# Four attention layers on one core: layer 1's neighbour rows fetched by an indirect DMA instead of one-hot products

## The reference, cut to what matters

```python
q = split(rmsnorm(x_tokens, gamma_q) @ Wq.T)              # 16 heads of 16
kn = rmsnorm(ctx, gamma_kv)
k, v = split(kn @ Wk.T), split(kn @ Wv.T)
mask = abs(ctx_pos - ctx_index_per_token) <= 1            # three rows per token
w = square(relu(q . k / 4)), zero outside the mask
out = (w / max(sum(w), 1e-6)) @ v
return x_tokens + out @ Wo.T
```

## Time and profile before

| | |
|---|---|
| median of three runs | 1463.18 us |
| the profiled execution | 1463.84 us |
| its span in the trace | 1462.0 us |
| TensorE busy | 1306.4 us, 89% |
| VectorE busy | 958.3 us, 66% |
| ScalarE busy | 779.8 us, 53% |
| GpSimd busy | 356.7 us, 24% |
| chain that ended last | TensorE 72%, VectorE 19%, ScalarE 4% |
| memory traffic | mean 20 GB/s over the span |

### The profile page before, as it was taken

How to read it: one execution, slowest core, us unless ns; L and a number is a source line. 1 busy time by engine, 2 the same in 40 slices (tenths; PEclk the granted TensorE clock), 3 DMA queues, 4 the chain that set the end, 5 groups by cost and what they waited for, 6 DMA issues and landing times.

```text
span 1462.0 us, 26277 instructions
## 1 busy us (share of the span) xinstructions
PE 1306.4 (89%) x9618; PEld 1027.6 (70%) x9618; DVE 958.3 (66%) x1908; ACT 779.8 (53%) x2690; POOL 356.7 (24%) x782
## 2 busy tenths in 40 slices
PE   3667889999999999999999999999999999888755
PEld 2345667877777787778777777877787777776533
DVE  2446567768686867777686768677776868573522
ACT  1133556657565646566575656464665656464411
POOL 1112303232322213132323232131323232302020
PEclk9779999999999999999999999999999999999855
DMA  6700000000000000000000000000000000000000
GB/s 205 282 1 13 3 12 2 17 4 16 4 16 4 9 11 0 20 0 16 4 16 4 16 4 9 11 0 20 0 16 4 16 4 4 4 5 5 4 4 4
DMA packets 23967, 28.65 MB, mean 20 GB/s; under 512 B 2144, under 2 KB 20096, under 8 KB 23424
## 3 DMA queue, kind: packets, MB, share of 16 engines
q1 hardware_dynamic: 23936, 28.24, 6.0%
HBM read 26.11 MB, written 2.13 MB: 19 GB/s over the span
## 4 chain that ended last, share of the span: by engine, by line
PE 72%; DVE 19%; ACT 4%; issue 3%; SPq 1%; DMA 0%; DVEq 0%; POOL 0%; another core or an unknown queue 0%; POOLq 0%; ACTq 0%
PE psum L477 44%; PE psum L471 8%; PE psum L660 4%; DVE small_ L1002 4%; PE psum L641 3%; PE psum L581 3%; DVE sa_p L996 3%; PE psum L693 2%; PE psum L705 2%; PE psum L525 2%; ACT sa_p L798 2%; ACT A L790 2%; DVE ca_p L1010 1%; PE psum L541 1%; PE psum L737 1%
## 5 line engine op out<-in xcount | busy, mean ns | idle before, releaser
L1286 POOL TENSOR_SCALAR small_<-small_ 128x1 f32<-128x1 f32 x112 | 36.0, 321 | 946.7 <-DVE small_ L1014 477.0
L790 ACT ACTIVATE A<-A,small_ 128x128 f32<-128x128 f32 x384 | 148.5, 389 | 91.0 <-DVE small_ L1003 91.0
L471 PE MATMUL psum<-cst,A 128*128 128x128 f32 x672 | 108.8, 289 | 59.1 <-DVE A L1010 36.7
L783 ACT ACTIVATE A<-psum 128x1024 f32<-128x1024 f32 (+2 forms) x112 | 76.5, 683 | 133.6 <-PE psum L471 125.2
L471 PEld LDWEIGHTS psum<-cst,A 128*128 128x128 f32 x672 | 80.6, 147 | 80.2 <-DVE A L1010 41.7
L1175 DVE SCALAR_TENSOR_TENSOR A<-psum,half_cw,A 128x127 f32<-128x127 f32 (+2 forms) x288 | 76.3, 340 | 68.4 <-ACT A L894 68.4
L790 ACT ACTIVATE ca_p<-ca_p,small_ 128x128 f32<-128x128 f32 x256 | 98.8, 394 | 4.9 <-DVE small_ L1003 4.9
L790 ACT ACTIVATE sa_p<-sa_p,small_ 128x128 f32<-128x128 f32 x256 | 98.8, 392 | 0.1
L783 ACT ACTIVATE sa_k<-psum 128x512 f32<-128x512 f32 (+1 forms) x48 | 35.5, 739 | 98.4 <-PE psum L477 53.5
L790 ACT ACTIVATION_READ_ACCUMULATOR A<-A,small_ 128x1 f32 x384 | 72.1, 188 | 0.0
L477 PEld LDWEIGHTS psum<-sa_p,Wsaq 128*128 128x128 f32 x512 | 58.8, 193 | 18.5 <-issue 18.5
(11 more groups left out here) (219 smaller groups left out, 3281.9 us busy)
## 6 DMA issues: line engine op xcount, KB each, us to landing
inT<-in_tokT SPq DMA_DIRECT2D x16, 256.0 KB, 2.7
ctx_in<-in_ctx SPq DMA_DIRECT2D x16, 128.0 KB, 2.1
A<-bias_rows SPq DMA_DIRECT2D x1, 2048.0 KB, 9.3
Wsakv<-in_wsa_kv SPq DMA_DIRECT2D x1, 2048.0 KB, 12.3
Wcakv<-in_wca_kv SPq DMA_DIRECT2D x1, 2048.0 KB, 13.3
ctx_end<-in_tokT SPq DMA_DIRECT2D x16, 128.0 KB, 2.2
out<-x_out SPq DMA_DIRECT2D x16, 128.0 KB, 1.7
Wmi<-in_wm_in SPq DMA_DIRECT2D x1, 1288.0 KB, 18.7
```

Source lines behind the costliest of these rows:

```text
L471: mm = pe.transpose(out[:, c * P:(c + 1) * P], src[:, c * P:(c + 1) * P], ident)
L783: return act.activation(out, in_, ACT.Copy)
L790: ins = act.activation(p[:, h * T:(h + 1) * T], p[:, h * T:(h + 1) * T], ACT.Exp, bias=sm(part, "nm", w * HU + h, w * HU + h + 1), accum_o ...
```

## The change

Layer 1's three rows per token are fetched by a gather from device memory. The keys and values of a batch (128 rows of 512 numbers) are stored by SP's queue to a table `kv_rows` in device memory, which has three extra rows at either end that are zeroed once at the start. GpSimd works out one offset per token (index + 2 rows, clamped), and starts one indirect DMA: each of the 128 tokens gets 1536 contiguous numbers, that is, its three neighbouring rows with keys and values (6 KB each, 768 KB in all). They land beside `kv1` in places that held layer 0's probabilities. The one-hot matrices and the six products with them are gone. VectorE now reads the neighbours from on-chip memory, in one instruction where there were two. The index is loaded as one number per partition instead of a row of 128 for all partitions. The strings of `ORDER` are new for all four engines.

```diff
@@ SP
+            def store_kv(made):
+                sp.wait_ge(sem["kv1_sb"], made)
+                sp.dma_start(kv_rows.ap()[EDGE:EDGE + T], kv1).then_inc(sem["kv_out"], 16)
             def load_next(b, passed):
-                sp.wait_ge(sem["onehot"], passed)
+                sp.wait_ge(sem["near_at"], passed)
                 load_idx(b)
                 sp.wait_ge(sem["out0T"], passed)
                 sp.wait_ge(sem["kv1"], passed)
                 load_tokens(b)
+                store_kv(passed)
                 sp.wait_ge(sem["cn_hat"], passed)
                 load_ctx(b)
@@ TensorE
-            def select(which, waits):
-                def run(t):
-                    need(t, *waits)
-                    kv = kv1[:, which * D:(which + 1) * D]
-                    for j in range(NEAR):
-                        mm = pe.matmul(P_1[:, j * D:(j + 1) * D], near[:, j * T:(j + 1) * T], kv, start=True, stop=True)
-                    mm.then_inc(sem[("sel_k", "sel_v")[which]], 1)
-                return run
@@ VectorE
-            def near_k(t):
-                need(t, "sel_k", "q1_sb")
...
+            def weights1(t):
+                dve.wait_ge(sem["near_in"], t.value(16, 16))
+                need(t, "q1_sb")
                 w, dn = sm(1, "w"), sm(1, "dn")
+                then(dve.tensor_tensor(prod..., near_k, spread(q1, NEAR), ALU.mult))
                 then(dve.tensor_reduce(w, prod.rearrange("p (a d) -> p a d", d=HD1), AX.X, ALU.add))
...
+            def mixed1(t):
+                then(dve.tensor_tensor(prod..., near_v..., w4, ALU.mult))
                 then(dve.tensor_tensor(o1, prod[:, 0:D], prod[:, D:2 * D], ALU.add))
                 dve.tensor_tensor(o1, o1, prod[:, 2 * D:3 * D], ALU.add).then_inc(sem["o1"], 1)
@@ GpSimd
-            def onehot(t):
...
+            def near_rows(t):
                 pool.wait_ge(sem["idx_in"], t.value(16, 16))
+                free(t, "x2")
                 held()
+                then(pool.tensor_scalar(near_at[:], idx_in[:], 2, 0, ALU.add, ALU.max))
+                pool.tensor_scalar(near_at[:], near_at[:], T + 3, 2 * D, ALU.min, ALU.mult).then_inc(sem["near_at"], 1)
+            def gather(t):
+                pool.wait_ge(sem["kv_out"], t.value(16, 3 * 16))
+                need(t, "near_at")
+                rows = bass.AP(tensor=kv_rows, offset=0, ap=[[1, (T + 2 * EDGE) * 2 * D], [1, 1]])
+                pool.indirect_dma_start(near, None, rows, bass.IndirectOffsetOnAxis(near_at[:, 0:1], 0)).then_inc(sem["near_in"], 16)
...
-                "inputs": [ctx_rstd], "attn0": [onehot], "back0": [rms0], "center0": [rms1],
+                "inputs": [ctx_rstd], "attn0": [near_rows], "near_q": [gather], "back0": [rms0], "center0": [rms1],
@@ ORDER, one of the four strings
-    "PE": "14314341312312343241321412413243141213414142321421414",
+    "PE": "314312434231314134232121413142443143142142321424141",
```

More of the change, by code:

```diff
@@ L11 @@
 HD0 = 16
-H1, HD1, NEAR = 16, 16, 3
+H1, HD1, NEAR, EDGE = 16, 16, 3, 3
 H2, HD2 = 16, 64
@@ L33 @@
 AX = mybir.AxisListType
-_CONSTS = [("ident", P), ("center", T), ("after", T), ("upto", T), ("window", T), ("quad", 4), ("pair", 2),
-           ("near", NEAR)]
+_CONSTS = [("ident", P), ("center", T), ("after", T), ("upto", T), ("window", T), ("quad", 4), ("pair", 2)]
 _SETUP = [("buckets", 2 * T - 1), ("flip", P)]
@@ L120 @@
 ORDER = {
[L121 to L124 removed]
+    "PE": "314312434231314134232121413142443143142142321424141",
+    "Activation": "434342134314141232113441323142123242441",
+    "DVE": "412121431444342134133214314442124124134111241",
+    "Pool": "4244141121132",
 }
@@ L144 @@
     "prep_exp", "prep_done", "bias_ps", "bias_sb", "skewed_in",
-    "kv0", "q0", "l0_o", "attnT", "gateT", "out0", "x1c", "x1T", "kv1", "q1", "sel_k", "sel_v", "o1T", "y1",
+    "kv0", "q0", "l0_o", "attnT", "gateT", "out0", "x1c", "x1T", "kv1", "q1", "o1T", "y1",
     "sa_hatT", "sa_q", "sa_k", "sa_v", "sa_oT", "sa_y", "ca_cT", "ca_hatT", "ca_q", "ca_k", "ca_v", "ca_oT", "ca_y",
@@ L170, in build @@
 def build(nc, tokT, ctx, idx, pad, cols, rows, consts, setup, rel, w0_q, w0_k, w0_v, w0_o, w0_g, w1_q, w1_kv, w1_o,
-          wsa_q, wsa_kv, wsa_o, wca_q, wca_kv, wca_o, wm_in, wm_out, w3_q, w3_k, w3_v, w3_o, bias_rows, out):
+          wsa_q, wsa_kv, wsa_o, wca_q, wca_kv, wca_o, wm_in, wm_out, w3_q, w3_k, w3_v, w3_o, bias_rows, kv_rows, out):
     with ExitStack() as stack:
@@ L234, in build @@
         probs0, PT0 = R(2), R(3)
-        kv1, near, idxf = R(2, 0, 2 * D), R(2, 2 * D, 2 * D + NEAR * T), R(2, 2 * D + NEAR * T)
-        prod, o1 = R(3, 0, NEAR * D), R(3, NEAR * D)
+        kv1 = R(2, 0, 2 * D)
+        near = A1[:].rearrange("p n m -> p (n m)")[:, 2 * UNIT + 2 * D:2 * UNIT + 2 * D + NEAR * 2 * D]
+        near_k, near_v = (near.rearrange("p (j n) -> p j n", j=NEAR)[:, :, a:a + D] for a in (0, D))
+        prod, o1 = R(0, 0, NEAR * D), R(1, D, 2 * D)
         xnT2, cnT2, hat2 = ({L: PB2[L][:, n * D:(n + 1) * D] for L in ("sa", "ca")} for n in range(3))
@@ L433, in _ @@
             weights("w0_in", [(W0q, w0_q), (W0k, w0_k), (W0v, w0_v), (W0o, w0_o), (W0g, w0_g)])
+            sp.wait_ge(sem["prep_done"], 2)
+            for a in (0, EDGE + T):
+                sp.dma_start(kv_rows.ap()[a:a + EDGE], Q2["ca"][0:EDGE, 0:2 * D]).then_inc(sem["kv_out"], 16)
             sp.wait_ge(sem["bias_sb"], 1)
@@ L453, in _ @@
                 store(i, sp.snap(i + 1))
+            store_kv(B)
             for b in range(B - 4, B):
@@ L1295, in ctx_rstd @@
                 pool.tensor_tensor(sm(1, "cr"), t1, neg_half[:], ALU.pow).then_inc(sem["ctx_rstd"], 1)
-            def onehot(t):
+            def near_rows(t):
                 pool.wait_ge(sem["idx_in"], t.value(16, 16))
-                need_unit(t, "l0_PT", 1)
+                free(t, "x2")
                 held()
-                then(pool.tensor_copy(idxf, idx_in[:]))
-                for j in range(NEAR):
-                    a = CONST_AT["near"][0] + j
-                    ins = pool.tensor_scalar(near[:, j * T:(j + 1) * T], idxf, cst[:, a:a + 1], None, ALU.is_equal)
-                ins.then_inc(sem["onehot"], 1)
+                then(pool.tensor_scalar(near_at[:], idx_in[:], 2, 0, ALU.add, ALU.max))
[5 more added lines that the diff above has]
+                pool.indirect_dma_start(near, None, rows, bass.IndirectOffsetOnAxis(near_at[:, 0:1], 0)).then_inc(sem["near_in"], 16)
             def rms0(t):
@@ L1447 @@
     bias_rows = nc.dram_tensor("bias_rows", (2 * H2, 2 * T - 1), F32)
-    build(nc, *args, bias_rows, out)
+    kv_rows = nc.dram_tensor("kv_rows", (T + 2 * EDGE, 2 * D), F32)
+    build(nc, *args, bias_rows, kv_rows, out)
     got = run_bass_kernel_spmd(nc, [arrays], core_ids=[0])
```

34 lines of the change are left out of this document (12 added, 22 removed).

## The result

| | before | after |
|---|---|---|
| median | 1463.1 us (1457.2 to 1464.1, four runs) | 1412.7 us (1411.8 to 1414.2, four runs) |
| span of the profiled execution | 1462.0 us | 1411.0 us |
| ratio | | 0.9664, 95% interval 0.9637 to 0.9691 |
| one turn of the loop, `kv0` to `kv0` | 80.20 us | 76.52 us |
| TensorE busy in one turn, and the rest | 77.75 and 2.45 us | 75.05 and 1.47 us |

A forecast was written before the change was run, and what follows sets the result against it. The loop was taken as bound by TensorE, busy 77.55 of 80.00 us. Loop -36.3, opening +3 and the two phases -1.5 sum to -34.8 us, from 1463.84 to 1429.0 us; range 1412 to 1465.

The forecast's parts named there:

- the case that had 0.05: Outcome beside the main forecast: waits shrink as well and the time is below 1418 us; chance 0.05.
- The gather is hidden: Loop: gather starts 1.5 us after x1, takes 6.2 of the 7.8 us before VectorE's scaled query, 1.6 left.
- The hold on GpSimd: Rival, chance 0.06: VectorE's on-chip products hold GpSimd before the gather; one hold stays hidden, two give 1435 us.
- the sharper form of the rival: GpSimd's descriptor writing stops while VectorE holds the shared port: 2.5 us more, gather 8.7 us, sum 1443 us.
- Each us beyond the slack costs one in every batch: Gather landing: each us beyond 7.8 costs one us in every batch, 16 in all.
- The rival of the late gather: VectorE waits for `near_in`, TensorE idles before o1's turn; gain gone from 10.0 us, 1501 us at 12.3; chance 0.20.
- The loop gains 2.79 us per turn; the waits cancel: Loop: removed products save 36.3 us over 13 turns; 0.9 us new waits, 1.8 us old ones and a few tenths cancel.
- Products are worth their time on TensorE: Six products per batch, 1.39 and 1.40 us on the bounding engine, counted in full as 2.79 us gained.
- The tail of layer 1 eats half: Rival, chance 0.11: late layer 3 probabilities delay o1, wait 2 us rather than 0.7; loop gains 18 us, time 1447.
- The opening, +3: Before the loop the gather is in the open: lands at 71.5 against 68.45, 3 us later (bounds 0 and 9).
- The two phases, -1.5: Two phases before the loop: 5.6 us of products go, but less other work covers; 1.5 us gain taken.
- The drains, 0 give or take 3: Three draining phases have no part 1 and only another order: 0 us, give or take 3.

The follow-up runs named there:

- the kernel with the old drains: Changed kernel with its three draining phases (those without part 1) in the merge order of the kernel before: 1416.7 us, ratio 0.9698.
- The order alone: Kernel before, one-hot products kept, put in the changed kernel's merge order: 1455.6 us, ratio 0.9957, turn 80.04 us.
- the fetch alone: Changed kernel with gathered rows, but in the merge order of the kernel before, less the two product stages: 1459.9 us, ratio 0.9982, turn 79.33 us.

## Why the prediction was right, and by how much

The direction was right. The range held by a narrow margin: 1412.7 us is 0.7 above its lower end, 1412, and the second measurement of the same kernel, 1408.1 us, lies below it. The gain was 51 us where 34.8 were forecast. The forecast's own range, 1418 to 1441, had the chance of 0.58 and was missed. What came is the case that had 0.05: waits shrink as well, and the time is below 1418. So the mechanism was found, and its size only just falls within the bounds.

- *The gather is hidden.* Right: it lands in 4.8 us (forecast 6.2) and has 7.2 us from its start (forecast 7.8). The estimate by the Trainium skill ("DMA: Bandwidth & Descriptors", Anatomy of one DMA) was 3.8 us, 1.0 us less than the trace has. The bound of 12.3 us from above was not the largest that the trace before offers: the same view has a load of 1288 KB with 18.7 us and one of 1024 KB with 16.7, both in the crowd of the weights. The hold on GpSimd happened, once per turn ahead of the gather: 0.95 us at 813.16, beside VectorE's product at 812.83, where the same operation takes 0.19 us elsewhere. The issue of the gather itself takes 1.09 to 1.22 us. That doesn't rule out the sharper form of the rival, which was never put to the test: beside an issue VectorE has only instructions with at most one large operand on chip (from 815.02 the scores out of the accumulators, then a sum), in every trace here.
- *Each us beyond the slack costs one in every batch.* Right for VectorE, too small for the kernel: 5.6 us of wait cost 7.6, since TensorE's granted clock was 0.50 behind the idle time. The rival of the late gather was priced too low by that.
- *The loop gains 2.79 us per turn; the waits cancel.* This is the mis-sized term: 2.79 us per turn forecast, 3.68 measured, or 36.3 us in 13 turns against 47.8 (the loop of the trace has 46.7). The two new waits came as worked out (0.54 ahead of the turn of o1, forecast 0.7; 0.29 ahead of `kv0`, forecast 0.2), and the old 1.07 and 0.71 us went. What failed is "I let these cancel". By the prediction's own numbers 1.8 us of waits go and 0.9 come, so 0.9 per turn are left over, and a few tenths elsewhere don't use them up. The few tenths came to one wait of 0.27 us and some 0.3 in small gaps, while two more waits of 0.3 us went. What was left is 0.89 us per turn.
- *Products are worth their time on TensorE.* The sum rested on this, and it was right only by the order beside it. With the old order they were worth 0.87 us, and the kernel would have been level with before. Each half alone gains 0.16 or 0.87 us of a turn, both 3.68. The prediction did not look at what waits beside the products in TensorE's queue; that the new order came with the change made its price come out.
- *The tail of layer 1 eats half.* It took 0.83 us in two waits, as in the forecast's own account. The probabilities of layer 3 end at 821.67, and the scaled query begins at 821.66, right behind them.
- *The opening, +3.* Right in the sum, by two errors that offset each other: VectorE begins at 71.23 us instead of 68.45, 2.8 us later. The gather started at 66.20, not at the root's end (65.05). Besides the offsets, which GpSimd had made at 38.9, it waits only for the store, and that was issued at 62.32: 3.9 us, where the prediction had 1.7 to 2.7. Against that it landed 1.4 us sooner than forecast. With the store issued ahead of the token load the first gather starts at 65.0 us, in the other kernels at 65.3 to 66.5; one trace doesn't show that this is the earlier store. In the changed kernel:

```profile
66.20 1.22 POOL L1301 DMA_INDIRECT A<-kv_rows,near_at  x1 [1.15 <-POOLq L1263]
```

- *The two phases, -1.5.* Not settled. Up to the second `kv0` of the loop, where the traces of the changed kernel agree, the forecast comes to +3 - 1.5 - 2.8 = -1.3 us. Measured are +0.4 in two traces and -1.6 in that of the kernel with the old drains, whose code is the same up to there; the granted clock differs between them. The wait for o1 stood there too:

```profile
215.17 0.44 PE L481 MATMUL psum<-cst,A 128*128 128x128 f32 x2 [2.32 <-DVE A L1102]
```

- *The drains, 0 give or take 3.* Mis-sized: -7.5. The order alone has drains of 195.3 us, the fetch alone 206.3, and over all traces the new strings take 7.6 us less than the old ones. The prediction had put nothing there, with no reason but that the drains have no part 1.

## What to carry to other kernels

Before pricing work that is taken off the full engine, look at what waits beside it in its queue: where the next instruction depends on another engine, the removed work was cover, and the price is what is left after the wait that appears. A change of data path and its new order are one change; try each half alone before crediting either. And a stall behind which TensorE's granted clock is lower costs more than its length: here 7.6 us for 5.6.

## What was not expected of the hardware

- An indirect DMA of 128 rows of 6 KB (768 KB), issued by GpSimd, lands 4.6 to 5.0 us after its start in all 16 blocks of the changed kernel, in the loop as in the opening; the other traces have 4.5 to 5.1, and one of them 6.3 at most. GpSimd itself is held 1.1 us. The load of 256 KB takes 2.9 us in the same trace.
- 6.4 us of idle time on TensorE were followed by a granted clock of 0.50 (820 to 825 us), then 0.89 (825 to 830). The wait of 2.3 us before the loop was followed by 1.00 in one trace of the changed kernel (220 to 225 us) and by 0.58 in the other (217 to 222 us); these two traces do not say on what that hangs.
